# Three scattered sends in flight, an early row number and an earlier normalisation in an attention and mixture-of-experts kernel

## The chip, the cores and the metric

The kernel runs on one core of one Trainium2 chip. The metric is the device time of one execution in microseconds (us), lower is better; the median of three executions stands for a kernel.

## What is computed

Four batches of 512 tokens with 256 features go through a cross attention with a residual, then through a mixture of eight experts, of which each token uses its best two. Cut to what matters:

```python
x = x + attention(layernorm(x), ctx)          # 4 x 512 x 256, single head of 256
xn = layernorm(x)
probs = softmax(xn @ Wr.T)                    # 8 experts
top_v, top_i = top_k(probs, 2); top_v /= sum(top_v)
for e in range(8):
    w_e = sum(where(top_i == e, top_v, 0))
    h = gelu(xn @ W1[e].T + b1[e])            # 1024 hidden
    out += (h @ W2[e].T + b2[e]) * w_e
x = x + out
```

## The kernel before

All engines run one hand-written order each and meet at semaphores. Names used below: PE multiplies, ACT is the scalar engine, DVE the vector engine, POOL the engine that issues scattered DMAs, SP the engine that issues most other DMAs.

The work has two halves. First the attention of batch b = 0 to 3 (128 tokens at a time, q = 0 to 3). After each batch DVE normalises its 512 rows a second time (`ln2_apply`, line 1163, result `xn2`), ACT writes the batch to `out` (`store`, line 974), PE turns the normalised rows and forms the router's logits, DVE picks two experts per token (`route_...`), PE counts how many rows of the batch go to each expert (`ranks`, lines 703 to 708), DVE turns the counts into row numbers (`place_next`, line 1377, to `place_sums`, line 1389). POOL then sends the 512 rows to `rows`, a DRAM table in order of experts: 8 indirect DMAs per batch, one for each of two choices k and four tiles q (`send_rows`, line 521). DVE needs `rstd`, the inverse deviation, for `ln2_apply`; POOL computes it (`rsqrt`, line 504) from `vare` of DVE (line 1158), and for the last batch that instruction stands in POOL's order between the sixth and the seventh send of the third batch (b = 2).

Then the experts: 24 tiles t of 128 or 256 rows. For each, SP reads from `row_of` at which row of `rows` the tile begins (`value_load`, line 426), loads the rows turned (`dma_start_transpose`, line 427, into `xT`) and their gates (line 429, into `xm`). PE does the first layer (`firsts`, line 790), ACT the gelu (line 1064), DVE splits the result into two 16-bit halves (`split`, `gh` at line 1687 and `gl` at line 1689), PE does the second layer (`seconds`, line 808), DVE adds the bias and multiplies by the gate (`result`, lines 1719 and 1723), POOL adds the result to `out` (line 555). The weights are split into 16-bit halves too: ACT makes the high half (line 949), DVE the low half in two instructions per weight unit (`low(u, k)`, line 1278), and SP and PE may go on when `low_ready` has counted the second one.

The tiles begin before the routing is over. Tiles 0 and 1 (128 rows) hold rows of batches 0 and 1 alone. Tile 2 (`MINI`) is the first of 256 rows and the first that needs the third batch: SP waits for `tables_ready` 2 (`early_done` of DVE, line 1511) and for all eight landings of that batch (line 444), then reads the row number, then issues the load. It next issues a 1 MB load of the second bias (line 447) and the loads of tiles 3 to 5. Tile 6 (`FIRST_LATE`) is the first that needs the fourth batch; its row number comes from `late_table` and `late_rows` of DVE (lines 1516 to 1556), which stand between splits in DVE's order.

"Paced" sends: POOL may have two sends of a batch in flight. The landings alternate between two semaphores of the batch, and each send waits until the one two places ahead has landed. The third batch (b = 2) is sent paced in program order: k = 0, q = 0 to 3; k = 1, q = 0 and 1; `rsqrt`; k = 1, q = 2 and 3.

Of the kernel before, what the change touches and what calls it, by code (L numbers as in the profile page):

```python
# [31 lines left out]
E, M = 8, 1024  # L32
# [3 lines left out]
QT = LQ // P  # L36
# [11 lines left out]
REGION = TR + N  # L48
# [10 lines left out]
MINI = -(-((B - 2) * LQ - FIRST_E * (P - 1)) // P)  # L59
# [22 lines left out]
TILES = expert_tiles()  # L82
# [12 lines left out]
def width(t):  # L95
    return P * halves(t)
# [42 lines left out]
def build(nc, x, ctxT, WqT, bq, WkT, WvB, WrT, W1T, b1, W2T, b2, rows, out):  # L139
    uses = projection_order()  # L140
    with ExitStack() as ctx:
# [3 lines left out]
        def sem(name):  # L145
            return ctx.enter_context(nc.semaphore(name))
# [11 lines left out]
        before = sb("before", [P, P], BF16)  # L158
# [158 lines left out]
        chosen_ready = sem("chosen_ready")  # L317
        gate_ready = sem("gate_ready")
        sent = [sem(f"sent{i}") for i in range(4)]
        staged_in = [sem(f"staged_in{i}") for i in range(RING + 1)]  # L320
        squared = sem("squared")
        scale_ready = sem("scale_ready")
# [43 lines left out]
        def _(sp):  # L366
# [48 lines left out]
                    load_ctx(3)  # L415


            def load_rows(t):
                if t >= XB:

                    sp.wait_ge(h_full, GROUPS[t - XB + 1])
                if t >= MB:

                    sp.wait_ge(added, 16 * BEFORE[t - MB + 1])
                slot, wide = TILES[t], width(t)
                first = sp.value_load(row_of[0:1, slot:slot + 1], min_val=0, max_val=E * REGION - wide)
                sp.dma_start_transpose(xT[:, t % XB, :, 0:wide],
                                       rows[bass.ds(first, wide), 0:D].bitcast(F16)).then_inc(xt_in[t % XB], 16)
                sp.dma_start(xm[:, t % MB, 0:halves(t), :],
                             rows[bass.ds(first, wide), D:ROW].rearrange("(h p) d -> p h d", p=P)).then_inc(meta_in[t % MB], 16)  # L430
# [9 lines left out]
            load_rows(1)  # L440

            sp.wait_ge(tables_ready, 2)
            for i in range(2):
                sp.wait_ge(sent[i], 16 * QT * 2)
            load_rows(MINI)
            sp.wait_ge(low_ready, UNITS - 1)
            sp.dma_start(b2_sb[:], b2.partition_broadcast(P)).then_inc(b2_in, 16)
            for t in range(MINI + 1, FIRST_LATE):
                load_rows(t)

            sp.wait_ge(tables_ready, 3)
            for i in range(4):
                sp.wait_ge(sent[i], 16 * QT * 2)
            for t in range(FIRST_LATE, NTILES):
                load_rows(t)
# [6 lines left out]
        def _(pool):  # L462
# [49 lines left out]
            def send_rows(b, k, tiles=range(QT), paced=False):  # L512

                pool.wait_ge(gate_ready, b + 1)
                pool.wait_ge(row_split, 2 * (b + 1))
                for q in tiles:
                    landing = sent[2 * (b % 2) + q % 2]
                    ahead = (k * QT + q) // 2
                    if paced and ahead:
                        pool.wait_ge(landing, 16 * (QT * (b // 2) + ahead))  # L520
                    pool.indirect_dma_start(out=rows, out_offset=bass.IndirectOffsetOnAxis(ap=place[:, b, k, q:q + 1], axis=0),  # L521
                                            in_=send[b % 2][:, q, :], in_offset=None).then_inc(landing, 16)

# [582 lines left out]
        def _(dve):  # L1106
# [167 lines left out]
            def low(u, k):  # L1274
                dve.wait_ge(high_ready, u + 1)
                hi, lo = unit_tiles(u)
                n = slice(k * M, (k + 1) * M)
                i = nc.vector.scalar_tensor_tensor(out=lo[:, n], in0=stages[STAGE[u]][:, n], scalar=up[:, u, 0:1].bitcast(F32),
                                                   in1=hi[:, n], op0=ALU.mult, op1=ALU.subtract)
                if k:  # L1280
                    i.then_inc(low_ready, 1)
# [288 lines left out]
            b = 0  # L1570
# [236 lines left out]
            scales_undo()  # L1807
            split(0, 1, e0)
            early_ats()
            low(u + 2, 0)  # L1810
            early_done()
            ln2_apply(b)
            low(u + 2, 1)
            e1 = expert(1)
            rows_high(b)
# [95 lines left out]
```

## Time and profile before

| | before |
|---|---|
| three executions, us | 347.18, 348.70, 354.43 |
| median, us | 348.70 |
| the profiled execution, us | 347.63 |
| its span (first to last instruction), us | 345.9 |
| PE busy, share of the span | 327.2 us, 95% |
| DVE busy | 258.4 us, 75% |
| ACT busy | 188.8 us, 55% |
| POOL busy | 120.2 us, 35% |
| mean granted TensorE clock | 0.991 of full |

All times below are us from the start of the span. The profiled execution took 1.7 us more than its span. A busy share says how much of the span an engine worked, not what the end waited for; for that one reads the chain of work that ended last, and then each engine's instructions in order of time around the places where the chain stands still.

### The profile page before, as it was taken

How to read it: one execution, taken by the hardware profiler on the slowest of the kernel's cores; microseconds unless marked ns; L12 is line 12 of the kernel's file. 1: busy time of each engine (PE TensorE's matmuls, PEld its weight loads, DVE VectorE, ACT ScalarE, POOL GpSimd, SP SyncE). 2: the span in 40 equal slices, each digit the busy share in tenths (PEclk: the TensorE clock that was granted, in tenths of full speed). 3: DMA queues.
4: the chain of work that ended last, by engine and by line, in shares of the span. 5: the costliest groups of instructions: out<-in, count | busy, mean ns of one | idle time of the engine just before them, and what ended most of it. 6: DMA issues, size and time to landing. Idle time of an engine off the chain costs nothing.

```text
span 345.9 us, 8734 instructions
## 1 busy us (share of the span) xinstructions
PE 327.2 (95%) x2648; PEld 268.1 (77%) x2648; DVE 258.4 (75%) x720; ACT 188.8 (55%) x333; POOL 120.2 (35%) x124
## 2 busy tenths in 40 slices
PE   7999999999999897999999999999999999999980
PEld 3557766767667776888778888989989898989870
DVE  4256999989989997888888677566767576767660
ACT  2489879979988865633442334343435353535220
POOL 6017211462371560447334322332332423131332
PEclk9999999999999999999999999999999999999996
DMA  7998975594785217643255424335424343344212
GB/s 222 369 351 259 245 265 184 180 293 131 241 284 154 79 66 221 94 88 62 48 79 70 60 42 63 49 40 56 62 34 63 37 60 46 51 54 56 32 17 30
DMA packets 51113, 41.82 MB, mean 121 GB/s; under 512 B 28542, under 2 KB 46527, under 8 KB 50943
## 3 DMA queue, kind: packets, MB, share of 16 engines
q1 hardware_dynamic: 40798, 27.36, 30.3%
q0 software_dynamic: 7872, 11.77, 19.2%
q10 hardware_dynamic: 2400, 2.13, 1.9%
q8 instruction: 26, 0.43, 0.6%
q14 instruction: 17, 0.13, 0.1%
HBM read 22.28 MB, written 13.86 MB: 104 GB/s over the span
## 4 chain that ended last, share of the span: by engine, by line
PE 69%; DVE 11%; ACT 9%; issue 4%; DMA 2%; SPq 1%; POOLq 1%; DVEq 1%; POOL 0%; ACTq 0%
PE o_ps L808 25%; PE s_ps L790 13%; PE t_ps L790 12%; PE s_ps L655 7%; PE proj L617 3%; DVE gl L1689 3%; PE o_ps L677 2%; ACT w1h L949 2%; ACT w1l L942 2%; PE proj L692 2%; PE proj L642 2%; DVE gh L1687 2%; PE proj L625 2%; DMA w1l<-WvB 1%; PE t_ps L665 1%
## 5 line engine op out<-in xcount | busy, mean ns | idle before, releaser
L555 POOL DMA_INDIRECT out<-y,xm x39 | 61.3, 1571 | 127.3 <-DVE y L1723 123.7
L1064 ACT ACTIVATE g<-s_ps,b_sb,down 128x256 f32<-128x256 f32 (+1 forms) x100 | 45.4, 519 | 79.9 <-PE s_ps L790 71.9
L808 PE MATMUL o_ps<-w2h,gh 128*128 x312 | 85.0, 273 | 1.0 <-DVE y L1719 1.0
L808 PE MATMUL o_ps<-w2h,gl 128*128 x312 | 85.0, 273 | 0.0
L808 PE MATMUL o_ps<-w2l,gh 128*128 x312 | 85.0, 272 | 0.0
L1687 DVE TENSOR_SCALAR gh<-g,up 128x512 f16<-128x512 f32 x78 | 38.3, 491 | 34.4 <-ACT g L1064 31.9
L1064 ACT ACTIVATE g<-t_ps,b_sb,down 128x256 f32<-128x256 f32 (+1 forms) x92 | 42.7, 524 | 38.2 <-PE t_ps L790 37.3
L1689 DVE SCALAR_TENSOR_TENSOR gl<-g,up,gh 128x512 f16<-128x512 f32 x78 | 58.6, 752 | 2.8
L790 PE MATMUL s_ps<-xT,w1h 128*128 128x256 f16 (+1 forms) x400 | 50.7, 252 | 2.7 <-issue 1.9
L790 PE MATMUL t_ps<-xT,w1h 128*128 128x256 f16 (+1 forms) x368 | 48.5, 255 | 0.0
L521 POOL DMA_INDIRECT rows<-send,place x32 | 33.9, 1061 | 31.1 <-DVE place L1389 19.1
L790 PEld LDWEIGHTS s_ps<-xT,w1h 128*128 x400 | 34.1, 98 | 6.8 <-issue 3.2
L808 PEld LDWEIGHTS o_ps<-w2h,gh 128*128 128x128 f16 x312 | 30.6, 98 | 6.0 <-DVE y L1719 1.6
L790 PEld LDWEIGHTS t_ps<-xT,w1h 128*128 x368 | 32.1, 98 | 3.8
L790 PE MATMUL s_ps<-xT,w1l 128*128 128x256 f16 (+1 forms) x200 | 34.2, 251 | 0.0
L808 PEld LDWEIGHTS o_ps<-w2l,gh 128*128 128x128 f16 x312 | 30.5, 98 | 3.5
L808 PEld LDWEIGHTS o_ps<-w2h,gl 128*128 128x128 f16 x312 | 30.5, 98 | 3.5
L790 PE MATMUL t_ps<-xT,w1l 128*128 128x256 f16 (+1 forms) x184 | 31.9, 254 | 0.0
L677 PE MATMUL o_ps<-v_sb,probsT 128*128 128x256 f32 x128 | 30.4, 383 | 0.2 <-ACT probsT L930 0.2
L1719 DVE SCALAR_TENSOR_TENSOR y<-o_ps,undo,b_sb 128x256 f32<-128x256 f32 x39 | 18.9, 483 | 12.0 <-PE o_ps L808 7.0
L677 PEld LDWEIGHTS o_ps<-v_sb,probsT 128*128 128x128 f32 x128 | 23.5, 190 | 5.1 <-issue 2.0
L504 POOL TENSOR_TENSOR rstd<-vare,half 128x4 f32<-128x4 f32 x8 | 9.8, 1220 | 36.7 <-DVE vare L1158 36.6
(226 smaller groups left out, 493.3 us busy)
## 6 DMA issues: line engine op xcount, KB each, us to landing
staged<-W2T SPq DMA_DIRECT2D x8, 1024.0 KB, 7.4
staged<-W1T SPq DMA_DIRECT2D x7, 1024.0 KB, 5.0
rows<-send POOLq DMA_DIRECT2D x8, 260.0 KB, 4.9
x_own<-x SPq DMA_DIRECT2D x2, 512.0 KB, 4.9
w2l<-W1T SPq DMA_DIRECT2D x1, 1024.0 KB, 10.5
out<-x_own ACTq DMA_DIRECT2D x2, 512.0 KB, 4.3
b_sb<-b SPq DMA_DIRECT2D x1, 1024.0 KB, 5.2
out<-y,xm POOLq DMA_INDIRECT x39
```

The costliest lines, as they stand in the source:

```text
L504: nc.gpsimd.tensor_tensor(rstd[:, which, b * QT:(b + 1) * QT], vare[:, which, b * QT:(b + 1) * QT], half[:, b * QT:(b + 1) * QT], ALU.pow) ...
L521: pool.indirect_dma_start(out=rows, out_offset=bass.IndirectOffsetOnAxis(ap=place[:, b, k, q:q + 1], axis=0), in_=send[b % 2][:, q, :], in ...
L555: pool.indirect_dma_start(out=out, out_offset=bass.IndirectOffsetOnAxis(ap=xm[:, t % MB, r, META - 1:META].bitcast(I32), axis=0), in_=y2[: ...
L617: i = nc.tensor.matmul(bank[:, 0:D], ctx_sb[b % 2][0:PART[t], t, k * P:(k + 1) * P], wv_sb[0:PART[t], t, :], start=(t == 0), stop=(t == 1))
L655: i = nc.tensor.matmul(s_ps[n % 2][:, 0:LK], qT[0:PART[c], c, q * P:(q + 1) * P], ctx_sb[b % 2][0:PART[c], c, :], start=(c == 0), stop=(c ...
L677: i = nc.tensor.matmul(o_ps[n % 2][:, 0:D], probsT[:, n % 2, k, :], v_sb[:, k, :], start=(k == 0), stop=(k == KT - 1))
L790: i = nc.tensor.matmul(h_ps[group % 4][:, to:to + width(t)], w[:, bass.ds(e, 1), at:at + P].rearrange("p a n -> p (a n)"), xT[:, t % XB, x ...
L808: i = nc.tensor.matmul(y_ps[n % 2][:, 0:D], l[:, t % 2, m, r * P:(r + 1) * P], w[:, bass.ds(e, 1), m * D:(m + 1) * D].rearrange("p a n -> ...
L1064: i = nc.scalar.activation(g[:, m, 0:width(t)], h_ps[group % 4][:, at:at + width(t)], ACT.Gelu, bias=b1_sb[:, bass.ds(e, 1), m:m + 1].rear ...
L1687: nc.vector.tensor_scalar(gh[:, t % 2, m, n], g[:, m, n], by, None, ALU.mult).then_inc(g_high, 1)
L1689: nc.vector.scalar_tensor_tensor(out=gl[:, t % 2, m, n], in0=g[:, m, n], scalar=by, in1=gh[:, t % 2, m, n], op0=ALU.mult, op1=ALU.subtract ...
L1719: nc.vector.scalar_tensor_tensor(out=y1[:, r, :], in0=y_ps[(BEFORE[t] + r) % 2][:, 0:D], scalar=undo[:, bass.ds(e, 1)], in1=b2_sb[:, bass. ...
```

## The change

Three edits.

1. The third batch's eight sends get three semaphores of their own, `third0` to `third2`, taken in turn, and each send waits for the one three places ahead. All other batches stay as they were. SP waits for the three instead of `sent0` and `sent1` (3, 3 and 2 landings), and later for `sent2` and `sent3` alone.
2. For tile 2 SP reads the row number ahead of the wait for the landings, not behind it (`first_row`, then `load_rows(MINI, first)`).
3. On DVE `ln2_apply` of the last batch moves ahead of `low(14, 0)`, a half of the low part of a weight unit (`u + 2` is 14 there); `low(14, 1)` stays where it was, directly behind.

```diff
+        third = [sem(f"third{i}") for i in range(3)]
...
+            def first_row(t):
+                return sp.value_load(row_of[0:1, TILES[t]:TILES[t] + 1], min_val=0, max_val=E * REGION - width(t))
+
+            def load_rows(t, first=None):
...
-                slot, wide = TILES[t], width(t)
-                first = sp.value_load(row_of[0:1, slot:slot + 1], min_val=0, max_val=E * REGION - wide)
+                wide = width(t)
+                if first is None:
+                    first = first_row(t)
...
             sp.wait_ge(tables_ready, 2)
-            for i in range(2):
-                sp.wait_ge(sent[i], 16 * QT * 2)
-            load_rows(MINI)
+            first = first_row(MINI)
+            for i in range(3):
+                sp.wait_ge(third[i], 16 * len(range(i, 2 * QT, 3)))
+            load_rows(MINI, first)
...
             sp.wait_ge(tables_ready, 3)
-            for i in range(4):
+            for i in range(2, 4):
                 sp.wait_ge(sent[i], 16 * QT * 2)
...
-                    landing = sent[2 * (b % 2) + q % 2]
-                    ahead = (k * QT + q) // 2
+                    if b == 2:
+                        landing, ahead, before = third[(k * QT + q) % 3], (k * QT + q) // 3, 0
+                    else:
+                        landing, ahead, before = sent[2 * (b % 2) + q % 2], (k * QT + q) // 2, QT * (b // 2)
                     if paced and ahead:
-                        pool.wait_ge(landing, 16 * (QT * (b // 2) + ahead))
+                        pool.wait_ge(landing, 16 * (before + ahead))
...
             early_ats()
-            low(u + 2, 0)
             early_done()
             ln2_apply(b)
+            low(u + 2, 0)
             low(u + 2, 1)
```

How the three places read in the engines' instructions. On POOL, the sends of the third batch before, with the semaphores that each waits for (the first two of the eight wait for no landing):

```order
L521 DMA rows<-send0,place 18432x260 [waits row_split,gate_ready]
L521 DMA rows<-send0,place 18432x260
L521 DMA rows<-send0,place 18432x260 [waits sent0]
L521 DMA rows<-send0,place 18432x260 [waits sent1]
L521 DMA rows<-send0,place 18432x260 [waits sent0,row_split,gate_ready]
L521 DMA rows<-send0,place 18432x260 [waits sent1]
L504 TENSOR_TENSOR rstd<-vare,half 128x4 [waits ln2_var]
L521 DMA rows<-send0,place 18432x260 [waits sent0,row_split,gate_ready]
L521 DMA rows<-send0,place 18432x260 [waits sent1]
```

And now:

```order
L529 DMA rows<-send0,place 18432x260 [waits row_split,gate_ready]
L529 DMA rows<-send0,place 18432x260 x2
L529 DMA rows<-send0,place 18432x260 [waits third0]
L529 DMA rows<-send0,place 18432x260 [waits third1,row_split,gate_ready]
L529 DMA rows<-send0,place 18432x260 [waits third2]
L510 TENSOR_TENSOR rstd<-vare,half 128x4 [waits ln2_var]
L529 DMA rows<-send0,place 18432x260 [waits third0,row_split,gate_ready]
L529 DMA rows<-send0,place 18432x260 [waits third1]
```

The order is the same; the waits look one send further back.

On SP, the load of tile 2 (`xT`) and what follows it, before (`b_sb<-b` is the load of the second bias):

```order
L426 TENSOR_LOAD row_of [waits sent1,h_full,sent0,tables_ready]
L426 ISA x2
L427 ISA
L427 DMA_TRANSPOSE xT<-rows 128x4x256
L429 ISA
L429 DMA xm<-rows 128x2x4
L447 DMA b_sb<-b 128x2048 [waits low_ready]
```

And now:

```order
L420 TENSOR_LOAD row_of [waits tables_ready]
L420 ISA x2
L432 ISA [waits third2,h_full,third1,third0]
L432 DMA_TRANSPOSE xT<-rows 128x4x256
L434 ISA
L434 DMA xm<-rows 128x2x4
L453 DMA b_sb<-b 128x2048 [waits low_ready]
```

The waits for landings moved from the read of the row number to the address instruction behind it.

On DVE, around the last `ln2_apply` (`xn<-x_own,mv,rstd`), between the splits of tile 0 and of tile 1, before:

```order
L1687 TENSOR_SCALAR gh<-g,up 128x4x128
L1689 SCALAR_TENSOR_TENSOR gl<-g,up,gh 128x4x128
L1507 TENSOR_REDUCE early_at<-early_row 128x4
L1278 SCALAR_TENSOR_TENSOR w1l<-staged,up,w1h 128x1024
L1511 TENSOR_TENSOR row_of<-early_at,slot_row 128x4
L1163 TENSOR_SCALAR xn<-x_own,mv,rstd 128x256 x4
L1278 SCALAR_TENSOR_TENSOR w1l<-staged,up,w1h 128x1024
```

And now:

```order
L1695 TENSOR_SCALAR gh<-g,up 128x4x128
L1697 SCALAR_TENSOR_TENSOR gl<-g,up,gh 128x4x128
L1515 TENSOR_REDUCE early_at<-early_row 128x4
L1519 TENSOR_TENSOR row_of<-early_at,slot_row 128x4
L1171 TENSOR_SCALAR xn<-x_own,mv,rstd 128x256 x4
L1286 SCALAR_TENSOR_TENSOR w1l<-staged,up,w1h 128x1024 x2
```

One weight half left its place ahead of `row_of` and `xn` and stands behind them.

## Rows read from the trace of the kernel before

**Rows 1.** The page: busy time of each engine, granted clock in 40 slices.
```profile
PE 327.2 (95%) x2648; PEld 268.1 (77%) x2648; DVE 258.4 (75%) x720; ACT 188.8 (55%) x333; POOL 120.2 (35%) x124
PEclk9999999999999999999999999999999999999996
```
**Rows 2.** Chain that ended last, in order of time: start us, us, what.
```profile
131.62 1.33 PE o_ps L808 x12
132.95 1.88 issue
134.83 2.81 PE s_ps L790 x24
...
172.03 3.17 DMA xT<-rows
175.34 2.84 PE s_ps L790 x24
```
**Rows 3.** SP's waits: engine line waited for: us in total, times, longest us.
```profile
SPq L444 <- DMA rows<-send,place: 15.2, 1, 15.2
```
**Rows 4.** SP's read of tile 2's row number, 128 to 131.3 us (ns, start).
```profile
L426 SPq TENSOR_LOAD <-row_of x1: 887/887/887, 130.0 to 130.0; - x1
```
**Rows 5.** SP in order of time: start us, us, engine line op.
```profile
131.28 1.77 SPq L427 DMA_TRANSPOSE xT<-rows  x1
```
**Rows 6.** POOL in order of time, from the third batch's second send [idle before <-releaser].
```profile
115.13 1.89 POOL L521 DMA_INDIRECT rows<-send,place  x1 [0.30 <-issue]
117.33 0.96 POOL L521 DMA_INDIRECT rows<-send,place  x1 [0.30 <-DMA rows<-send,place]
118.77 0.95 POOL L521 DMA_INDIRECT rows<-send,place  x1 [0.48 <-DMA rows<-send,place]
120.79 1.35 POOL L521 DMA_INDIRECT rows<-send,place  x1 [1.06 <-issue]
123.57 0.96 POOL L521 DMA_INDIRECT rows<-send,place  x1 [1.43 <-DMA rows<-send,place]
124.56 1.17 POOL L504 TENSOR_TENSOR rstd<-vare,half 128x4 f32<-128x4 f32 x1
125.92 1.09 POOL L521 DMA_INDIRECT rows<-send,place  x1 [0.20 <-issue]
127.32 0.99 POOL L521 DMA_INDIRECT rows<-send,place  x1 [0.30 <-issue]
```
**Rows 7.** DVE in order of time.
```profile
121.81 0.30 DVE L1158 TENSOR_SCALAR vare<-mv 128x4 f32<-128x4 f32 x1
...
124.83 1.28 DVE L1278 SCALAR_TENSOR_TENSOR w1l<-staged,up,w1h 128x1024 f16<-128x1024 f32 x1
126.03 0.16 DVE L1511 TENSOR_TENSOR row_of<-early_at,slot_row 128x4 int32<-128x4 f32 x1
126.10 1.38 DVE L1163 TENSOR_SCALAR xn<-x_own,mv,rstd 128x256 f32<-128x256 f32 x4
...
133.37 0.49 DVE L1687 TENSOR_SCALAR gh<-g,up 128x512 f16<-128x512 f32 x1 [1.07 <-ACT g L1064]
...
141.78 0.19 DVE L1377 TENSOR_TENSOR next_at<-proj,nextrow 128x32 f32<-128x32 f32 x1 [0.66 <-PE proj L708]
```
**Rows 8.** PE in order of time.
```profile
127.53 1.09 PE L625 MATMUL proj<-ident,xn 128*128 128x128 f32 x8 [0.86 <-DVE xn L1163]
```
**Rows 9.** DVE's waits, 141.8 to 171.4 us.
```profile
DVE gh L1687 <- issue: 1.0, 2, 0.6
DVE y L1719 <- DVE gates L1704: 0.6, 3, 0.2
```
**Rows 10.** PE's waits, 175.4 to 334.8 us.
```profile
PE s_ps L790 <- DMA xT<-rows: 0.8, 1, 0.8
```
**Rows 11.** ACT's store of the last batch: its issue, and its queue in 129.5 to 131.2 us.
```profile
128.72 0.38 ACTq L974 DMA_DIRECT2D out<-x_own  x1
q10 hardware_dynamic: 515, 0.52, 89.3%
```

More of the change, by code:

```diff
@@ L415, in _ @@
                     load_ctx(3)
-            def load_rows(t):
+            def first_row(t):
+                return sp.value_load(row_of[0:1, TILES[t]:TILES[t] + 1], min_val=0, max_val=E * REGION - width(t))
+            def load_rows(t, first=None):
                 if t >= XB:
```

## The prediction

> **What bounds the kernel now.** I begin with the busy shares and the clock on the page: PE works 95% of the span, and its granted clock stands at full speed but for the last slice [rows 1]. So neither the clock nor one engine's total decides; the question is where PE stands still or waits. Next comes the chain that ended last [rows 2]. Before tile 2 it runs through many engines in short pieces; from 175.34 it is PE to the end, and the only wait of PE in the 159 us after that row is one of 0.8 us, the last part of the arrival that the row itself shows [rows 10]. Whatever starts the piece at 175.34 earlier therefore shortens the kernel by as much, and the change has to be judged by that start.
>
> Between the two the chain shows two standstills. PE has nothing at 132.95 to 134.83, and at 172.03 the chain is the 3.17 us load of tile 6, whose row number is the last result of DVE's late tables. "Issue" at 132.95 hides a transfer: the next PE work is the first layer of tile 2, whose rows SP began to load at 131.28 [rows 5]. SP had waited for landings [rows 3] and read the row number at 130.0, which took 0.89 us [rows 4]. The landings end POOL's series of sends [rows 6].
>
> Then I read each engine in order of time. PE stands 0.86 us before it turns the last batch's rows, for `xn2` of DVE [rows 8]. DVE idles 1.07 us at 132.30 to 133.37, for a gelu of ACT, and 0.66 us before `next_at` at 141.78, for PE's counts [rows 7]. From there to 171.4, where the late tables are done, DVE waits only 1.6 us in all, in pieces of up to 0.6, on its own gates and on issue [rows 9]. So **from 141.8 to the late tables DVE is the bound**, and what the change is worth at the end is what it makes `next_at` earlier.
>
> **The change part by part.**
>
> Sends, before: the eighth ends on POOL at 127.32 + 0.99 = 128.31 and SP goes on at 130.0, so a landing is seen 1.7 us after POOL's end. By that measure the second (end 117.02) would release at 118.7, which is when the fourth begins (118.77). The fourth ends at 119.72, but its successor by two begins at 123.57 and not at 121.4 or at the fifth's end: one straggling landing cost about 1.1 us there (the fifth ended at 122.14, plus 0.3 between two sends).
>
> Sends, now: the third is where it was, 117.33, since it waited for nothing but issue. The fourth waits for the first, long landed: 117.33 + 0.96 + 0.30 = 118.59. With a mean length L of one send on POOL the sixth ends at 117.33 + 4 L + 3 x 0.30. L over the last six sends is (0.96 + 0.95 + 1.35 + 0.96 + 1.09 + 0.99) / 6 = 1.05, so 122.43. `rstd` needs `vare`, done at 122.11 [rows 7], so it isn't held: 0.03 later it starts, and ends at 123.63, against 125.73. Sends seven and eight: 123.63 + 0.20 + 1.05 + 0.30 + 1.05 = 126.23. Each waits for a landing three back; the seventh for the fourth, in the rows seen by 123.3 to 123.6 even with its straggler. The bounds: no idle but 0.3 and sends of 0.95 give 125.6; the 1.06 us idle that the fifth had (unexplained "issue") coming again gives 127.0. I take 126.2, near what the mean says.
>
> Row number: `row_of` was done at 126.19; without the half weight ahead of it, at 125.1 (124.83 + 0.16, and 0.1 for its wait on `early_at`, which the half weight hid). SP's read then ends by 126.0 even at 0.89 us, before the landings at 126.2 + 1.7 = 127.9. Behind the landings only the address instruction is left, under 0.2 us. Before, landing to load was 131.28 - 130.0 = 1.28 us, so this saves 1.1 us, if the read is indeed finished by then. The load starts at 128.05, against 131.28. It took 134.83 - 131.28 = 3.55 us to PE's start, so rows are there at 131.6.
>
> One collision: ACT's 512 KB store of the last batch kept 16 queues 89% busy for 1.7 us, 1.5 us of all of them, and was over when tile 2's load moved its rows [rows 11]. The store comes 0.86 us earlier (below), the load 3.2: they now overlap. It adds 0 to 1.5 us; I take half, 0.75, since the two share the engines and the store begins first: 132.35.
>
> Normalisation: the low half costs 1.20 us (124.83 to 126.03) and goes behind. `xn` starts after `row_of`, at 125.1 instead of 126.10 (`rstd` is there at 123.63), and ends at 126.45. PE's previous piece ends at 127.53 - 0.86 = 126.67, so the idle 0.86 us goes whole, and everything to the end of the piece that began at 131.62 comes 0.86 us earlier: PE is free for tile 2 at 132.95 - 0.86 = 132.09. The moved half delays DVE's next split: from `xn`'s start to the end of the gates was 132.30 - 126.10 = 6.20, now 6.20 + 1.20 = 7.40, so 132.5, where ACT's gelu is ready at 133.37 - 0.86 = 132.51. The delay fits just inside the 1.07 us in which DVE stood idle; without that cover it would cost up to 1.2.
>
> Sum at DVE: from 133.37 on DVE comes 0.86 us earlier, and reaches `next_at` at 141.78 - 0.66 - 0.86 = 140.26 if PE's counts are ready. These ended 141.76 - 134.83 = 6.93 us after tile 2's start: 132.35 + 6.93 = 139.3. So the threshold is a tile 2 that starts by 133.3; I have it at 132.35, and **the gain at `next_at` is 1.5 us** (0.86 + 0.66), not the 2.5 us that PE gains. The late tables, tile 6's load and PE's piece at 175.34 come 1.5 us earlier with it. The loads of tiles 3 to 5 come earlier than before too and were not waited for. The remaining waits of the third batch's landings (SP, before tile 6) were over 40 us before.
>
> 347.63 - 1.5 = **346.1 us**. The profiled execution lies 1.1 us under the median of 348.70 and between the two lower ones; I keep to it, and leave the distance to the median in the range.
>
> **A rule against it.** The seventh send stood beside `xn` (125.92 to 127.01 against 126.10 to 127.48) and took 1.09 us, 0.1 more than its neighbours, and `xn` took no visible harm [rows 6, 7]. Now the eighth send, and not the seventh, is the one beside `xn` (125.1 to 126.5). The Trainium skill (SBUF — State Buffer, "SBUF: two separate sides") says that VectorE in certain fast modes and GpSimd hold a shared port alone for a whole instruction, so that descriptors of a POOL DMA can't be written meanwhile. By that rule the eighth send would end up to 1.3 us later and tile 2 start at 133.65, which makes the sum 347.63 - 1.2 = 346.4 us instead of 346.1. The row shows no such hold, and speaks against it.
>
> **Rivals.**
>
> A. Part of the gain: tile 2 arrives late. If the load stands behind the whole store (+1.5 us) and the eighth send behind the whole of `xn` (it would start at 126.45 instead of 125.18, +1.3), tile 2 starts at 131.6 + 1.5 + 1.3 = 134.4 and the gain is 134.83 - 134.4 = 0.4; either alone gives 133.1 or less and costs nothing. The middle between 133.3 and 134.4 is 133.9, which gives 0.9: 346.7 us. The hold by `xn` is the case of the Trainium skill's page above. Or `rstd` is no earlier than before (125.73): `xn` starts 0.65 late, the gates end at 133.15, and the gain is 133.37 - 133.15 + 0.66 = 0.9 again. For it: the unexplained 1.06 us. Against: in both the margins are near 1 us.
>
> B. It does nothing: sends land as before, since the waits were not what spaced them (two of four idle pieces read "issue"), and tile 2 starts at 134.8 or little earlier: 347.6 us. Against: the 0.88 us read of the row number goes in any case.
>
> C. Slower: POOL's sends get longer with three in flight. The second took 1.89 us. By the steps above the eighth ends at 119.93 + 6 L, the load starts 1.85 later, tile 2 another 3.55 later: 125.3 + 6 L. It is slower than before from L = 1.6 on. With all at 1.89 tile 2 starts at 136.7, 1.8 us late, PE's counts and `next_at` with it: 347.63 + 1.8 = 349.4 us. For it: the 1.89 and the 1.35. Against: the third to eighth had a mean of 1.05 with at most one other in flight, and the slow second one had only the first beside it, as it will have again.
>
> D. More: PE's 2.5 us come through whole, 345.1 us. Against: DVE's rows from 141.8 on, with 1.6 us idle in 30 [rows 9].
>
> **How the numbers follow.** Forecast 0.58, A 0.20, B 0.10, C 0.07, D 0.05. The range 345.0 to 348.9 holds the forecast, A, B, D and the milder half of C, and a median that lies 1.1 us above the profiled execution once more. Two per cent, about what a measurement of this kernel can tell from no change, is 7 us; no case comes near. Faster by more 0.02, within 0.95, slower by more 0.03, the last two hundredths for a cause that I don't see.
>
> **What would show it.** In the new profile: `rstd` at 122.4 to 123.6, the eighth send over near 126.2, tile 2's load issued near 128.0 with no read of the row number just before it, no idle time on PE before the turned rows, DVE's split of tile 1 at 132.5, PE at tile 2 between 132.1 and 133.3, `next_at` at 140.3 with no wait for PE's counts, the late load at 170.5, and PE's last long stretch from 173.8. The argument is wrong if `next_at` is early but PE's last stretch isn't, or if tile 2 starts after 133.3.

## The result, and the profile after

| | kernel before | changed kernel |
|---|---|---|
| median of 12 executions | 349.02 us | 350.03 us |
| lowest, highest | 347.05, 356.31 | 348.67, 350.75 |
| ratio (interval) | | 1.0049 (1.003 to 1.0068) |
| profiled execution, its span | 347.63, 345.9 | 350.42, 348.7 |

Forecast was 346.1 us, in a range up to 348.9: the time lies above both, and the sign is the other one. It is within 2% all the same. The ratios leave out executions more than 1.5% above the fastest, and since 77 of 117 executions of the kernel before on three chips and 7 of 35 on another were above 351 us, and none of 48 of the changed kernel, medians and ratios don't say the same, and both are given.

The page of the changed kernel, in answer to [rows 1]:

```profile
PE 330.2 (95%) x2648; PEld 269.7 (77%) x2648; DVE 259.3 (74%) x720; ACT 189.3 (54%) x333; POOL 120.4 (35%) x124
PEclk9999999999998989999999999999999999999997
```

PE is busy 3.0 us longer with the same 2648 instructions, and two slices have a lower granted clock. By stretch (its length, then busy us and count of instructions of PE, PEld, DVE, ACT, POOL, then the granted clock, the DMA share and GB/s), first before, then after; the last row is a second half-clock stretch, from 125.4:

```profile
101.00:109.00 8.00, 8.00 (x46) 5.88 (x45) 7.97 (x35) 6.46 (x14) 2.00 (x2) 1.00 0.77 247
```
```profile
101.00:109.00 8.00, 8.00 (x36) 5.08 (x35) 7.07 (x32) 5.20 (x10) 1.80 (x2) 0.79 0.76 248
...
125.00:129.00 4.00, 4.00 (x40) 3.83 (x40) 2.31 (x5) 3.59 (x11) 2.00 (x2) 0.57 0.20 69
```

The first stretch lies ahead of everything that the change touches: for 3.4 us TensorE had its lower level (1.2 instead of 2.4 GHz), 36 matmuls got through instead of 46, and all that follows is 1.36 us late (the third batch's first send stands at 115.16, before at 113.80). That much of the 2.8 us between the two spans is not the change's. The chain that ended last, for [rows 2]:

```profile
119.06 1.28 ACT L1051
120.55 3.93 another core or an unknown queue
...
174.69 3.31 DMA xT<-rows
178.13 1.93 PE s_ps L798 x16
```

There are 3.93 us at 120.55 that the chain of before did not have. POOL, SP, DVE and ACT in order of time, in answer to [rows 3 to 7]:

```profile
122.52 1.06 POOL L529 DMA_INDIRECT rows<-send,place  x1 [0.30 <-issue]
123.64 1.04 POOL L510 TENSOR_TENSOR rstd<-vare,half 128x4 f32<-128x4 f32 x1
...
126.54 0.97 POOL L529 DMA_INDIRECT rows<-send,place  x1 [0.30 <-issue]
```
```profile
130.29 1.26 SPq L432 DMA_TRANSPOSE xT<-rows  x1
```
```profile
123.25 0.30 DVE L1166 TENSOR_SCALAR vare<-mv 128x4 f32<-128x4 f32 x1
126.61 0.49 DVE L1695 TENSOR_SCALAR gh<-g,up 128x512 f16<-128x512 f32 x1 [3.06 <-ACT g L1072]
...
129.41 1.38 DVE L1171 TENSOR_SCALAR xn<-x_own,mv,rstd 128x256 f32<-128x256 f32 x4
130.70 2.48 DVE L1286 SCALAR_TENSOR_TENSOR w1l<-staged,up,w1h 128x1024 f16<-128x1024 f32 x2
...
144.39 0.18 DVE L1385 TENSOR_TENSOR next_at<-proj,nextrow 128x32 f32<-128x32 f32 x1
```
```profile
120.35 0.20 ACT L1051 ACTIVATE warm<-warm 128x1 f32<-128x1 f32 x1
124.80 2.63 ACT L1072 ACTIVATE g<-s_ps,b_sb,down 128x128 f32<-128x128 f32 x7 [4.24 <-remote]
```

Take 1.36 us off each of them and the steps of the edits are there: the eighth send is over at 126.15 (it was 128.31), `rstd` starts at 122.28 (124.56). But `xn`, whose inputs are done, starts at 128.05 instead of earlier than 126.10, because DVE stood still for 3.06 us ahead of tile 0's first split: ACT began its first GELU 5.8 us after PE's first product of tile 0 (119.03). PE meanwhile went on and then stuttered:

```profile
122.99 0.22 PE L798 MATMUL t_ps<-xT,w1h 128*128 128x128 f16 x1 [0.20 <-issue]
123.71 0.22 PE L798 MATMUL t_ps<-xT,w1h 128*128 128x128 f16 x1 [0.51 <-issue]
124.43 0.27 PE L798 MATMUL t_ps<-xT,w1l 128*128 128x128 f16 x2 [0.50 <-issue]
```

The 24 products that the first GELU needs had been issued by 120.4. The signal `h_full` that tells ACT so came at 124.5, and the next, due 24 products later, 0.23 us behind it. So by the trace it was not the products that were late but the news of them. Below, this late first GELU is called the standstill.

### The profile page after: what moved, and what is told of

Its sections match the earlier page's. It is cut to its first block, busy times and chain, and to the rows that moved or that the text cites. A ratio compares the mean times of both kernels' runs of the same rounds, so it can differ in the third digit from the quotient of the medians.

```text
span 348.7 us, 8733 instructions
## 1 busy us (share of the span) xinstructions
PE 330.2 (95%) x2648; PEld 269.7 (77%) x2648; DVE 259.3 (74%) x720; ACT 189.3 (54%) x333; POOL 120.4 (35%) x124
## 4 chain that ended last, share of the span: by engine, by line
PE 67%; DVE 12%; ACT 10%; issue 4%; another core or an unknown queue 1%; DMA 1%; POOL 1%; POOLq 1%; DVEq 1%; ACTq 0%; SPq 0%
PE o_ps L816 23%; PE s_ps L798 12%; PE t_ps L798 11%; PE s_ps L663 7%; DVE gl L1697 3%; PE proj L625 3%; PE o_ps L685 2%; ACT w1h L957 2%; DVE gh L1695 2%; ACT w1l L950 2%; PE proj L650 2%; PE o_ps L589 2%; PE proj L700 2%; ACT w2h L957 2%; PE t_ps L673 1%
## 5 line engine op out<-in xcount | busy, mean ns | idle before, releaser
L798 PE MATMUL t_ps<-xT,w1h 128*128 128x256 f16 (+1 forms) x368 | 49.5, 259 | 0.7 <-issue 0.7
L798 PEld LDWEIGHTS t_ps<-xT,w1h 128*128 x368 | 33.1, 100 | 3.7 <-issue 0.3
```

Of the source, the lines that this page charges most:

```text
L798: i = nc.tensor.matmul(h_ps[group % 4][:, to:to + width(t)], w[:, bass.ds(e, 1), at:at + P].rearrange("p a n -> p (a n)"), xT[:, t % XB, x ...
```

## The experiments

Four edits recur below. The changed kernel is 1, 2 and 3 together.

```
1  + third = [sem(f"third{i}") for i in range(3)]          (sends of batch 2 wait three back)
   + landing, ahead, before = third[(k*QT + q) % 3], (k*QT + q) // 3, 0
2  + first = first_row(MINI)                               (SP, ahead of the landing waits)
3  - low(u + 2, 0)                                         (DVE)
     early_done()
     ln2_apply(b)
   + low(u + 2, 0)
late store:
   - store(b)                                              (ACT, ahead of take_logits(b))
   + if t == MINI: store(B - 1)                            (ACT, behind tile 2's GELUs)
unpaced (on the changed kernel):
   - if paced and ahead:
   + if paced and ahead and b != 2:
```

**The kernel before again, and each edit alone (one chip).** The kernel before beside them: 352.52 us median, fastest 346.71 (29 executions).

> The kernel before, unchanged, as a run of its own, to see its clock and its places in a second profile. Theory chance (the 3.4 us stretches at half clock and PE's standstill at 120 to 124 us come and go between executions of any version): the granted clock scatters between 0.979 and 0.991 as in the changed kernel, and the span with it. Theory edit (one of the three edits brings them): every fast execution has a clock of 0.99 or above and a span near 345.9, and no half-clock stretch before the end; ratio 1.000.

Measured 352.48 us (347.16 to 356.27), profiled at 352.54.

> Edit 1 alone: three sends of the third batch in flight. If this edit is what makes PE stand still behind tile 0 (more software sends moving while PE begins the experts), the ratio is 1.005 or more and the profile shows the wait of ACT for tile 0 of over 3 us again. If it is another edit, the sends end some 2 us earlier and the time is 0 to 0.7 us shorter: ratio 0.998 to 1.000.

349.23 us (347.25 to 350.65), ratio 0.9935 (0.9896 to 0.9974).

> Edit 3 alone: the last normalisation ahead of the weight half. rstd comes no earlier than before (125.7), so DVE should stand some 0.65 us, and by the steps of the prediction the gain at next_at is limited by tile 2's start, which is where it was: 0. If this edit is the cause of the loss (DVE late for tile 1's split, which the theory of the lost cover says), the ratio is 1.003 to 1.007; otherwise 0.999 to 1.001.

353.47 us (351.5 to 354.03), ratio 1.0051 (1.0009 to 1.0092).

> Edit 2 alone: the row number read ahead of the landing wait. Tile 2's load starts 1.1 us earlier (130.2 instead of 131.3), PE's counts and next_at up to 0.66 us earlier: ratio 0.998 to 1.000 if the chain of the prediction holds. If the loss comes with any shift of the program in time or of its code, ratio above 1.002 here too.

352.39 us (348.69 to 353.62), ratio 1.0082 (1.0031 to 1.0132).

Only edit 1 gains here. Edits 2 and 3 alone leave the median within 1 us of the kernel before and have two of 12 and none of 12 executions under 351 us, where the kernel before has 10 of 29. What edit 1 removes is in the profile of the kernel before run again (POOL, DVE, SP, PE; queue rows: packets, MB, share of 16 engines, 130 to 134 us), which is not the execution that the prediction was made from:

```profile
128.26 1.81 POOL L521 DMA_INDIRECT rows<-send,place  x1 [0.30 <-issue]
127.97 1.27 DVE L1278 SCALAR_TENSOR_TENSOR w1l<-staged,up,w1h 128x1024 f16<-128x1024 f32 x1
135.25 1.26 SPq L427 DMA_TRANSPOSE xT<-rows  x1
138.79 1.03 PE L790 MATMUL s_ps<-xT,w1h 128*128 128x256 f16 x4 [5.28 <-issue]
```
```profile
q10 hardware_dynamic: 528, 0.52, 39.8%
q0 software_dynamic: 48, 0.13, 10.2%
```

The eighth send takes 1.81 us instead of 0.99 and is over at 130.07, when ACT's 512 KB store is moving; most of its rows land behind the store, tile 2's load leaves 4 us later than in [rows 5], and PE stands 5.28 us. The 0.8 us more has a cause in the rows: the send began 0.29 us into a weight half (`low`) of DVE, and ended 0.84 us behind that half's end at 129.23; in [rows 6] it began at 127.32, 0.07 us before the same half. `rstd` met the half before in the same way (2.01 us instead of 1.17). In the profile of edit 1 alone the eighth send was over at 126.62, 1.71 us long for the same reason, and tile 2 began at 134.63. Edits 2 and 3 leave the late send of 1.81 us as it is: their profiles have tile 2 at 138.16 and 139.38.

**Pairs of edits, and the late store (a second chip).** The kernel before there: 348.60 us median, fastest 346.68 (35 executions).

> The changed kernel once more, for a second profile. If the late start of tile 0's gelu (124.8 us, 4 us behind PE's first-layer matmuls) belongs to the changed kernel, it is there again and the executions lie between 348.6 and 350.8. If it was a matter of that execution, the gelu starts at 119.2 to 120.8 as in the kernels with one edit, and tile 2 starts at 132 to 133.5 (plus 1.4 where the clock was halved at 105 us). In either case none above 351, against about half of the executions of before.

349.71 us (348.62 to 350.89), ratio 1.0043 (1.0019 to 1.0067): the first result again.

> Edits 1 and 2 without the moved normalisation. With edit 1 the eighth send is over before the store of the last batch begins, so no execution above 351. If the moved normalisation (which brings the store 0.9 us forward) costs something, this is 0.3 to 1.5 us below the changed kernel, with executions down to 346.5; if not, the same as the changed kernel.

350.02 us (349.6 to 353.33), ratio 1.0071 (1.0042 to 1.01). Four of the 12 were above 351 us, where I had expected none.

> Edits 1 and 3 without the early row number: should lie between edit 1 alone (347.2 to 350.7) and the changed kernel (348.7 to 350.8). If it is like the changed kernel, the moved normalisation is what takes the low end away; if like edit 1 alone, it is the row number.

349.33 us (347.45 to 350.83), ratio 1.0027 (0.9998 to 1.0057).

> The kernel before, with the last batch's 512 KB store issued after the gelu of tile 2 instead of before the logits. Theory store (executions of before above 351 are those in which the eighth send's rows stand behind the store on the same queues, 1.7 us, and then behind an instruction load): none of the executions is above 351 any more, median 347 to 349, ratio 0.985 to 0.995, and the eighth send's rows move 0.6 us after POOL is done with it. Theory clock alone (they are only a matter of half-clock stretches): executions above 351 in half of the cases as before.

347.23 us (346.65 to 351.08), ratio 0.999 (0.9963 to 1.0017). The slowest execution is the profiled one: its eighth send is again 1.81 us long, and tile 2's load leaves 2.3 us behind it instead of 5.2 as in the run above. So the store was the larger part of that delay, and not the whole.

All three with edit 1 had the standstill: first GELUs with 4.22 to 4.26 us of idle ACT ahead of them. The kernel with only the late store did not (its first GELU came 1.8 us after the first product). Up to 0.9 us behind tile 0's first product the traces of edits 1+2 and of edit 1 alone (its second profile, below) agree to 0.01 us on PE, DVE, ACT and POOL, when neither edit 2 nor 3 has yet been reached. So I held that a second edit was needed and could not see how it could be.

**Is it the kernel? (a third chip.)** Before: 353.44 us median, fastest 346.91.

> Edits 2 and 3 without edit 1 (two sends in flight). Theory A (the standstill at tile 0, the first GELU only 5.8 us after the tile's first product, comes from the third batch's sends running back to back while tile 0 starts, which is edit 1's doing, and from one thing more): here the first GELU follows within 1.8 to 2.8 us as before the change, and the slower executions of the kernel before (351.5 us and more) are still there, so the median is within 0.5% of a median of 352 us where before has it, or a ratio of 1.000 to 1.010. Theory B (any two edits together shift the work so that it appears, whatever the sends do): the first GELU is 5.5 to 6 us late here too. Next rows of tile 2 loaded after 134 us in the profile by A, as in the runs of edit 2 and of edit 3 alone.

351.41 us (348.01 to 354.0), ratio 1.0088 (1.0035 to 1.0141); first GELU 1.8 us after the first product.

> Edit 1 alone a second time. Its first profile showed the first GELU 1.8 us after tile 0's first product and one half-clock stretch, at 134.9 us; its executions lay in two groups, 347.2 to 349.3 and 350.5 to 350.7 us. Theory A (the standstill comes in some executions of any kernel with edit 1, and the first profile was one without): the profile shows it, or not, by chance, and the times lie in the same two groups, about 2 us apart. Theory B (it needs the second edit): no standstill, the first GELU 1.8 to 2.8 us after the first product. By both no execution above 351 us, and a ratio of 0.990 to 1.002 depending on how many executions of the kernel before are of its slow kind.

348.85 us (347.4 to 350.76), ratio 0.9958 (0.9912 to 1.0004); first GELU at 1.8 us.

> Edit 1 with the last attention batch's 512 KB store issued after tile 2's GELUs instead of before the logits, so that it lies beside none of the sends or tile 2's load. Theory A (the store beside the eighth send and the load is what is left of tile 2's lateness): the load of tile 2 is on the rows at 128 to 129 us and landed by 132.5, the half-clock stretch behind PE's standstill goes, and the time is 345.5 to 347.5, below both kernels. Theory B (the lead is taken back by what else tile 2 waits for, the split of tile 1 and PE): same as edit 1 alone, 347.5 to 349.5.

346.72 us (346.22 to 348.68, 6 executions), ratio 0.9875 (0.9812 to 0.9938), tile 2 at 133.29.

> The changed kernel with no landing waits at all among the third batch's eight sends. Theory A (sends back to back beside tile 0 hold up PE's signals to ACT): the sends' instructions move earlier still, the standstill at tile 0 stays at 5.5 to 6 us after the first product or moves to an earlier place, and the time is 349 to 352. Theory B (the sends' timing has nothing to do with it): the standstill stays where it is to within 0.2 us, the eighth send is over about 1 us earlier, and the time is 348.5 to 350.

350.01 us (346.44 to 350.58), ratio 1.0013 (0.995 to 1.0075); first GELU at 1.8 us. Neither theory had this. Its first six sends stand at the same distances from tile 0's start (to 0.03 us) as those of the changed kernel, and yet there was no standstill.

**The changed kernel on the first chip again.** Before: 352.92 us median, fastest 346.80.

> The changed kernel a third time, on another chip. Theory A (the standstill at tile 0 belongs to this kernel): the first GELU again 5.7 to 5.8 us after tile 0's first product, next_at at 143.0 or, with a half-clock stretch at 105, 144.4, all executions between 348.6 and 350.9. Theory B (it belongs to the chip or the execution): the first GELU 1.8 us after, as in the unpaced kernel on chip 7, xn at 124.5 to 126, tile 2 by 133 to 134.9, and some executions at 345.5 to 347.5, which no execution of the changed kernel has had so far (24 executions, the fastest 348.62).

348.46 us (346.52 to 350.38), ratio 1.0007 (0.9972 to 1.0042).

> The changed kernel without landing waits among the third batch's sends, a second time. Its first profile had no standstill at tile 0. Theory A (it is the waits or the instructions of the changed kernel that bring it): none here, whatever the run of the changed kernel beside it shows. Theory B (chip or execution): the same as in changed_third on the same chip, both with it or both without. Time 346.4 to 350.6 by both, as before.

348.68 us (347.28 to 350.53), ratio 1.0015 (0.9971 to 1.006). The landing waits of the changed kernel cost nothing.

> The changed kernel with the last attention batch's 512 KB store issued behind tile 2's GELUs. If the store beside the eighth send and tile 2's load was what held tile 2: tile 2's load landed by 132.5, no PE standstill before it, and the time 1.5 to 2.5 us below changed_third. Against edit 1 with the late store (346.72 median, 346.22 to 348.68): by theory A the standstill at tile 0 takes 1.2 us of it again, 347.5 to 349; by theory B the same or up to 0.7 us less, 345.5 to 347.

347.62 us (346.3 to 348.63), ratio 0.9975 (0.9936 to 1.0013).

Theory B held: the same kernel, no standstill. The changed kernel here (ACT, POOL, DVE, PE, SP):

```profile
119.48 1.57 ACT L1072 ACTIVATE g<-s_ps,b_sb,down 128x128 f32<-128x128 f32 x4 [0.31 <-ACT warm L1051]
```
```profile
122.25 1.22 POOL L510 TENSOR_TENSOR rstd<-vare,half 128x4 f32<-128x4 f32 x1
...
125.05 1.08 POOL L529 DMA_INDIRECT rows<-send,place  x1 [0.30 <-issue]
```
```profile
124.88 1.38 DVE L1171 TENSOR_SCALAR xn<-x_own,mv,rstd 128x256 f32<-128x256 f32 x4
...
132.59 0.49 DVE L1695 TENSOR_SCALAR gh<-g,up 128x512 f16<-128x512 f32 x1 [0.32 <-ACT g L1072]
...
143.14 0.19 DVE L1385 TENSOR_TENSOR next_at<-proj,nextrow 128x32 f32<-128x32 f32 x1 [2.79 <-PE proj L716]
```
```profile
134.52 0.62 PE L798 MATMUL s_ps<-xT,w1h 128*128 128x256 f16 x4 [2.35 <-issue]
```
```profile
127.76 1.26 SPq L432 DMA_TRANSPOSE xT<-rows  x1
```

This is the forecast, step for step, up to one row: the load leaves at 127.76, but PE gets tile 2's rows only at 134.52, 6.76 us later, where [rows 5] and [rows 2] gave 3.55. PE then stands 2.35 us for them and DVE, ready for `next_at` at 140.35, waits 2.79 us for PE's counts. The queues show with what the load shared its time. Before, in 132 to 135 us; the changed kernel, in 129 to 134; with the late store besides, in 130 to 134:

```profile
q1 hardware_dynamic: 1340, 0.36, 69.5%
```
```profile
q1 hardware_dynamic: 1347, 0.42, 67.4%
q10 hardware_dynamic: 528, 0.52, 31.5%
```
```profile
q1 hardware_dynamic: 1384, 0.73, 79.0%
```

Queue q1 has the load's 1,024 packets of 256 bytes, and some of the gates and the bias. Before, the load's packets began to move when the store's (q10) were all over. Now the load starts together with the store, and the store's half megabyte and the load's small packets go through the same 16 engines in turns. The Trainium skill (DMA: Bandwidth & Descriptors, "Rules for kernel authors") says that transfers from SP, ACT and GpSimd all run on the same 16 engines and interleave; the rows agree, and show the price for the one with small packets. With the late store (its own file has the lines one further down):

```profile
129.29 1.26 SPq L432 DMA_TRANSPOSE xT<-rows  x1
```
```profile
134.29 0.62 PE L798 MATMUL s_ps<-xT,w1h 128*128 128x256 f16 x4 [0.58 <-issue]
```
```profile
141.81 0.18 DVE L1386 TENSOR_TENSOR next_at<-proj,nextrow 128x32 f32<-128x32 f32 x1
```

This execution had a half-clock stretch at 106, ahead of everything here; its first send is at 115.37, against 113.78 in the changed kernel beside it, so 1.59 us come off: tile 2 at 132.70 and `next_at`, no longer waiting for PE, at 140.22. The load takes 5.00 us to PE instead of 6.76: **by these two runs the store's part is 1.8 us**. The packets agree: the first 1,000 of the load took 3.04 us beside the store, 1.28 with the late store, 1.32 before the change.

What is left, 5.00 instead of 3.55, goes with one more transfer, a single 16 KB packet of the queue that the profile calls instruction. It stands in the same two windows, first of the changed kernel, then with the late store, and not in that of the kernel before:

```profile
q8 instruction: 1, 0.02, 1.2%
```
```profile
q8 instruction: 1, 0.02, 1.8%
```

With the late store it ran from 131.86 for 1.14 us. Fifteen of the load's sixteen landing signals came by 132.58, the last at 134.09, and PE began 0.20 us behind that. In the changed kernel it ran from 131.72 for 0.93 us, and the last of the load's packets began 1.30 us behind the thousandth, where 0.21 us was the distance before. In the thirteen of the twenty profiles in which no such packet ran while the load's packets moved, the load took 3.2 to 3.6 us from issue to its last landing; in the seven in which one did, 4.4 to 6.7 us. Two of the seven have no store beside it (4.44 and 4.80 us). No run has the store beside the load without this packet, and none moves the packet by itself, so that the two shares are differences between runs.

**Does edit 1 alone bring the standstill? (a fourth chip.)** Before: 352.10 us median, fastest 346.83.

> The changed kernel a fourth time. If the standstill at tile 0 goes with the chip, this profile has it or not, and with it the times: with it the first GELU 5.7 to 5.8 us after tile 0's first product and no execution under 348.6 us; without it 1.8 us after, and the fastest executions at 346.5 to 347.6 us.

348.97 us (348.25 to 350.53), ratio 1.002 (0.9985 to 1.0055). The standstill is back.

> Edit 1 alone beside it. If the standstill needs only edit 1 and such a chip, it is here wherever changed_fourth has it; if it needs a second edit, it is not here although changed_fourth has it. If changed_fourth does not show it, none here, and a median of 348.5 to 349.3 as twice before.

351.30 us (349.51 to 354.88), seven of 12 above 351, ratio 1.0058 (1.0015 to 1.01). Here too, with edit 1 alone:

```profile
124.82 0.22 PE L793 MATMUL t_ps<-xT,w1h 128*128 128x128 f16 x1 [1.19 <-issue]
```
```profile
125.21 1.22 ACT L1067 ACTIVATE g<-s_ps,b_sb,down 128x128 f32<-128x128 f32 x3 [4.16 <-remote]
```

> Edit 1 with the store of the last attention batch behind tile 2's GELUs. The first time 346.72 us median (346.22 to 348.68), about 1.7 us under the changed kernel on the neighbouring chip. The same again: median 346.3 to 347.6, none above 349, below both kernels on the same chip.

351.53 us (349.67 to 355.2), ratio 1.0081 (1.0032 to 1.013), where the same kernel had 346.72 on the third chip. A miss by 5 us: its profile has the standstill at tile 0 and then PE at its lower level of clock for 10 us (same columns as above):

```profile
133.00:139.00 6.00, 6.00 (x32) 5.23 (x30) 3.50 (x8) 2.99 (x5) 0.00 (x0) 0.50 1.21 232
```

So the standstill goes with the chip and edit 1: of the profiles with edit 1, the seven on the second and fourth chips and in the first measurement all have it, the seven on the first and third have not. That edit 1 is needed rests on less: of kernels without it only two were profiled where the others have the standstill. The late store alone on the second chip has none, and the first profile of the kernel before has a small one (ACT idle):

```profile
120.46 2.97 ACT L1064 ACTIVATE g<-s_ps,b_sb,down 128x128 f32<-128x128 f32 x8 [1.27 <-PE s_ps L790]
```

There the first GELU was 2.8 us behind the first product, not 1.8. The other executions say the same: the fastest of the changed kernel was 348.25 to 348.67 us on chips with the standstill and 346.52 on the one without, while the fastest of the kernel before was 346.68 to 347.05 on all.

**What the standstill costs.** The fourth chip's profile of the changed kernel had no half-clock stretch before the end, so it can be laid beside [rows 7] as it is:

```profile
124.70 0.48 DVE L1695 TENSOR_SCALAR gh<-g,up 128x512 f16<-128x512 f32 x1 [2.96 <-ACT g L1072]
...
127.49 1.38 DVE L1171 TENSOR_SCALAR xn<-x_own,mv,rstd 128x256 f32<-128x256 f32 x4
```

Tile 0 begins at 117.28 here and at 117.65 on the first chip, so `xn` comes 10.2 us behind it instead of 7.2: the standstill takes 3.0 us, and DVE no longer waits for PE at `next_at`. That comes at 142.45, 25.2 us behind tile 0's start, where the kernel before (117.67, 141.78) had 24.1. A loss of 1.1 us; the span is 346.7 against 345.9.

## Why the prediction was wrong

- **What bounds, and where it is decided: right.** In every profile the end follows `next_at`: the span less that instant is 203.8 to 204.6 us in all twenty profiles.
- **Sends: right.** "So 122.43" for the end of the sixth and 126.23 for the eighth: measured 122.20 and 126.13 (125.05 + 1.08) on the first chip. The eighth beside `xn` took 1.08 us against 0.99 before, 0.1 us more and not the 1.3 that the rule against the forecast allowed. But "The row shows no such hold" misread the rows. In the twenty profiles 148 sends begin inside a weight half of DVE (1.28 us). Of these, 129 end 0.83 to 0.91 us behind the half's end, wherever in it they began, and take up to 2.06 us; the other 19 began at most 0.07 us behind its start and take 0.96 or 0.97. The seventh send in [rows 6] is one of the 129 (it ends 0.91 us behind the half that began at 124.83). `xn` is four instructions of 0.41 us: the eighth send began 0.17 us into the first and ended 0.84 us behind the end of that one. So the rule of the Trainium skill (SBUF — State Buffer, "SBUF: two separate sides"), by which certain VectorE instructions and those of GpSimd share a port, and whichever begins first keeps it for its whole instruction, agrees with the trace, and the price is set by the one instruction that the send meets. The same holds for the 1.89 us of the second send, which the prediction took for a sign that sends in flight get longer: it began 0.23 us into such a half.
- **Row number: right.** Load forecast at 128.05, measured 127.76.
- **Normalisation: right.** `xn` at 125.1 forecast, 124.88 measured; the next split at 132.5 forecast, 132.59 measured; DVE ready for `next_at` at 140.26 forecast, 140.35 measured. That the moved half weight just fits into DVE's idle time held: of 1.07 us 0.32 is left.
- **The collision: wrong, a term mis-sized.** "It adds 0 to 1.5 us; I take half, 0.75." Load to PE took 6.76 us instead of 3.55, 3.2 more; 1.8 of it is the store's and 1.45 goes with the 16 KB instruction packet, for which the sum had no term. With the store alone PE would have begun tile 2 at 127.76 + 3.55 + 1.76 = 133.07, an estimate from these rows, and the threshold of 133.3 would have held. So tile 2 starts at 134.52, behind my own threshold of 133.3, and by my own 6.93 us the counts come at 141.5: in the unpaced kernel, which had no half-clock stretch, tile 2 at 134.65 gave `next_at` at 141.60. The 3.5 us of lead are worth 0.3 us at tile 2 and 0.2 at `next_at`. That is rival B by A's mechanism: without the standstill the changed kernel is the kernel before (346.52 against 346.80 for the fastest). The mistake was to read 3.55 us off a load that ran when no other transfer was in the queues, and move it to a time when two were. With the store out of the way `next_at` is at 140.22, as forecast for the sum, and the fastest executions are at 346.3.
- **No term for PE's news to ACT.** In three of the four measurements of the changed kernel the standstill takes `xn` 3.0 us back, more than the 1.2 that the edits had given it (124.88 against 126.10). Nothing in the rows of before said that it would; the 1.27 us at 120.46, which I had not read, was the only sign. This is what turned no gain into a loss of about 1 us.
- **The profiled execution taken as typical.** "I keep to it, and leave the distance to the median in the range." It was one of the better executions of the kernel before, in which the eighth send was 0.99 us long, since it began 0.07 us ahead of DVE's weight half. In the profile of the same kernel on the first chip it is 1.81, with PE idle for 5.28 us. No profile with three sends in flight has that: tile 2 starts by 137.6 in all but one of them (140.84, the miss on the fourth chip), and the changed kernel's median is 348.46 against 352.92 on the first chip and 348.97 against 352.10 on the fourth, edit 1's 349.23 against 352.52 and 348.85 against 353.44, though on the fourth only 351.30 against 352.10. This gain I had not seen.
- **Half-clock stretches** had no place in the sum either. Each is worth 1.4 to 1.7 us: 1.36 in the first send of the changed kernel's profile, and 1.67 in the time from tile 2's start to PE's counts (8.24 us in the changed kernel on the first chip, with such a stretch at 135.4, against 6.57 in the unpaced kernel without one). They come before and after the change, and in some executions of one kernel and not in others, so that I don't put them down to the change.

No version beats both kernels on every chip. Edit 1 with the late store was the best where there is no standstill (346.72 us) and among the worst where there is (351.53); the changed kernel with the late store (347.62 us, first chip) has not been run on a chip with it. What stays open is the cause of the standstill: why PE's signals reach ACT 4 us late on some chips in kernels with edit 1. The kernel without landing waits, whose sends have the same spacing, was run only on chips without it. The traces from the second and fourth chips and of the first measurement also hold fewer records of landings (2244 to 2329, the kernel before in [rows 6] 2266) than those from the first and third (2666 to 2685). All seven profiles with the standstill are among those with fewer records, and so is the one with the small one, so that the recording and not the chip may be what differs; whether the two belong together was not tried.

## What to carry to other kernels

A load's duration belongs to the moment at which it ran: before moving it, lay its new window over every other transfer, instruction packets too, and where it would meet a long one, price it by the bytes of both through the same queues, or move the long one too. Before calling a scattered send long or short, see which VectorE instruction it began in: beside the weight halves here it ended 0.8 to 0.9 us behind the half's end. Run the kernel before more than once, and on more than one chip, before taking its profile as the base of a sum: here one profile hid both the late send that the change removes and a signal that was already 1 us late. And when a change ahead of a bound is made, check what is between it and the bound on a second chip, since 1 us there can be 3 on another.

## What the runs showed that I had not expected

- The same kernel, with traces that agree to 0.01 us on PE, DVE, ACT and POOL up to tile 0, waits 4.1 to 4.3 us for PE's first signal on some chips and 0.3 us on others; its two signals then come 0.23 us apart, and PE's own issue falls to one matmul in 0.72 us until they are out.
- A transposing load of 1,024 packets of 256 bytes and a 512 KB store that start together, with a 16 KB instruction packet behind: 6.76 us from issue to use, against 5.00 without the store and 3.55 with neither.
- The instruction packet took 0.93 to 1.17 us itself in the seven profiles in which it met the load, and one of the load's sixteen landings came 1.51 us behind the other fifteen (132.58 and 134.09, the changed kernel with the late store).
- A scattered send that began 0.05 us into a 1.26 us weight half of DVE took 2.06 us (edits 2 and 3); one that began 0.03 us into such a half took 0.96 (the kernel before).
- Ahead of the end of the program a granted clock of 0.5 lasted 3.4 us each time, and 10.2 us once (133.0 to 143.3, edit 1 with the late store on the fourth chip), after PE had been idle for 2.27 us.
